# A chunked scan over image rows: TensorE's products regrouped, cumulative sums copied inside SBUF, statistics every fourth row

## The reference

```python
dA_cs = jnp.cumsum(dA, axis=2)
Lmat = jnp.exp(dA_cs[:, :, :, None, :] - dA_cs[:, :, None, :, :])
att = jnp.einsum('bcihn,bcjhn->bcijh', Ch, Bh) * Lmat * dtc[:, :, None, :, :]
att = jnp.where(causal[None, None, :, :, None], att, 0.0)
y_intra = jnp.einsum('bcijh,bcjhp->bcihp', att, xc)
states = jnp.einsum('bcjhn,bcjh,bcjhp->bchpn', Bh, decay_to_end * dtc, xc)
y_inter = jnp.einsum('bcihn,bcih,bchpn->bcihp', Ch, jnp.exp(dA_cs), prev_states)
```

## Time and profile before

| | us |
|---|---|
| median of 3 runs | 2463.56 (2460.02 to 2467.26) |
| profiled execution, its own time | 2459.31 |
| its span, first to last instruction | 2457.5 |
| the scan, first to last work on TensorE | about 858 to 1835 |

### The profile page before, as it was taken

How to read it: one execution, slowest core, us unless ns; L and a number is a source line. 1 busy time by engine, 2 the same in 40 slices (tenths; PEclk the granted TensorE clock), 3 DMA queues, 4 the chain that set the end, 5 groups by cost and what they waited for, 6 DMA issues and landing times. The chain is left out here.

```text
span 2457.5 us, 64304 instructions
## 1 busy us (share of the span) xinstructions
PE 2165.3 (88%) x22969; PEld 1624.6 (66%) x23096; DVE 1662.4 (68%) x3164; ACT 1311.9 (53%) x2727; POOL 1109.5 (45%) x1392
## 2 busy tenths in 40 slices
PE   0699997998899399999999999999987999879998
PEld 0475645887788267777777777777766656356563
DVE  5355585665565578888888888888873555735557
ACT  0255540085047577777777777777743555334543
POOL 0333250000000168888778877878853322432325
PEclk9999997999999699999999999999998999989999
DMA  9624495415623422222222222222226045961459
GB/s 215 182 81 79 100 329 160 122 29 179 204 54 125 137 51 60 60 58 58 58 61 59 61 58 58 58 59 60 59 60 180 25 88 139 311 184 35 91 132 316
DMA packets 305629, 272.25 MB, mean 111 GB/s; under 512 B 175966, under 2 KB 238846, under 8 KB 299210
## 3 DMA queue, kind: packets, MB, share of 16 engines
q1 hardware_dynamic: 294698, 256.00, 37.5%
q0 software_dynamic: 9280, 6.44, 2.1%
q10 hardware_dynamic: 1496, 7.63, 1.0%
HBM read 165.29 MB, written 81.46 MB: 100 GB/s over the span
## 5 line engine op out<-in xcount | busy, mean ns | idle before, releaser
L1692 DVE TENSOR_TENSOR l_scan_att<-l_scan_decay,l_scan_causal_scores 128x512 f32<-128x512 f32 x384 | 330.2, 860 | 63.3 <-ACT l_scan_decay L1661 63.1
L715 ACT COPY l_arena<-l_body_bank 128x384 f32<-128x384 f32 x192 | 142.0, 901 | 262.3 <-PE l_body_bank L587 262.3
L1655 ACT ACTIVATE l_scan_decay<-l_scan_cum 128x512 f32<-128x512 f32 x384 | 216.3, 597 | 33.0 <-PE l_scan_cum L1547 32.9
L1661 ACT ACTIVATE l_scan_decay<-l_scan_decay 128x512 f32<-128x512 f32 x384 | 227.8, 630 | 4.1
L1672 ACT ACTIVATE l_scan_yw<-l_scan_y_by_channel,l_scan_norm_b,l_scan_norm_w 128x128 f32<-128x128 f32 x384 | 148.1, 456 | 125.5 <-PE l_scan_y_by_channel L1609 124.5
L1594 PE MATMUL l_scan_gate_projected<-l_scan_xr,l_wf 97*128 97x128 f32 (+1 forms) x1536 | 205.3, 283 | 1.4 <-DVE l_scan_xo L1747 1.2
L1625 PE MATMUL l_scan_gate_projected<-l_scan_yz,l_scan_wo 128*96 128x128 f32 x1536 | 198.5, 279 | 1.1 <-DVE l_scan_yz L1724 1.1
L567 POOL TENSOR_TENSOR l_arena<-l_arena 96x512 f32<-96x512 f32 x96 | 122.6, 1277 | 168.8 <-ACT l_arena L780 161.6
L1625 PEld LDWEIGHTS l_scan_gate_projected<-l_scan_yz,l_scan_wo 128*96 128x96 f32 x1536 | 170.9, 163 | 40.0 <-issue 29.6
L1512 POOL TENSOR_TENSOR l_scan_inter<-l_scan_inter,l_scan_xd 128x384 f32<-128x384 f32 x128 | 128.0, 1000 | 151.4 <-DVE l_scan_inter L1707 151.4
L1594 PEld LDWEIGHTS l_scan_gate_projected<-l_scan_xr,l_wf 97*128 97x128 f32 (+1 forms) x1536 | 181.0, 190 | 17.2 <-issue 2.2
(11 more groups left out here) (191 smaller groups left out, 4896.2 us busy)
## 6 DMA issues: line engine op xcount, KB each, us to landing
l_scan_xc<-convolved_rows SPq DMA_DIRECT2D x128, 224.0 KB, 2.8
x_after<-l_arena SPq DMA_DIRECT2D x64, 384.0 KB, 4.8
l_arena<-x_after SPq DMA_DIRECT2D x64, 384.0 KB, 5.6
convolved_rows<-l_slots SPq DMA_DIRECT2D x48, 441.0 KB
l_conv_x_main<-x_after SPq DMA_DIRECT2D x64, 256.0 KB, 2.8
l_arena<-x_after SPq DMA_DIRECT2D x16, 1024.0 KB, 8.7
prepare_xt<-x SPq DMA_DIRECT2D x8, 1536.0 KB, 9.3
l_arena<-x SPq DMA_DIRECT2D x32, 384.0 KB, 5.5
```

Of the source, the lines that this page charges most:

```text
L715: nc.scalar.copy(tA[:, b, :, j:j + 2].rearrange("p c q -> p q c"), bank[n % 4][:, 0:2 * C].rearrange("p (q c) -> p q c", q=2)).then_inc(t_ ...
L1655: nc.scalar.activation(decay[:, b % 2, 4 * g:4 * g + 4, :], cum[(b + g) % 2][:], ACT.Relu, scale=-1.0)\
L1661: nc.scalar.activation(group, group, ACT.Exp, scale=-1.0).then_inc(exp_done, 1)
L1692: nc.vector.tensor_tensor(att[:, b, 4 * g:4 * g + 4, :], decay[:, b % 2, 4 * g:4 * g + 4, :], causal[:, b % 2:b % 2 + 1, :].broadcast_to([ ...
```

## The change

In `step_sizes` the unused columns of `parts` are filled with -1 instead of 0, and so the unused partitions of `cum_t` hold -1. `pick` and `unpick` go. In their place `lift` holds, for each of the four rows in flight, the spreading weights, and three further partitions of it get the row's own cumulative sums (three bf16 parts, 12 heads of 128) by three DMAs from `cum_t` to `lift` inside SBUF. The partitions of -1 multiply these, so that four products of 128 columns give both terms and L1544's product of 512 columns is gone. The first cumulative group of a row waits for the three DMAs of that row.

```diff
@@ -1275,7 +1275,7 @@
 
             @block.gpsimd
             def _(pool):
-                nc.gpsimd.memset(parts[:], 0.0).then_inc(padded, 1)
+                nc.gpsimd.memset(parts[:], -1.0).then_inc(padded, 1)
...
-        pick = ph.sb("pick", [128, 2 * N_HEADS, 128], BF16)
-        unpick = ph.sb("unpick", [128, 2 * N_HEADS, 128], BF16)
+        lift = ph.sb("lift", [128, U, N_HEADS, 128], BF16)
...
-        xo = ph.sb("xo", [CH, U, 2, W])
+        xo = ph.sb("xo", [CH, 2, U, W])
...
-        half_i = slice(0, D_INNER // 2)
+        half_i, half_s = slice(0, D_INNER // 2), slice(D_INNER // 2, D_INNER)
...
+        lift_landed = [ph.sem(f"own_cum_landed{b}") for b in range(U)]
...
                     sp.dma_start(tile[:], source).then_inc(ready, 16)
+                sp.wait_ge(ready, CONST)
...
@@ -1461,6 +1462,12 @@
                             .then_inc(xc_landed[b], 16)
                         sp.dma_start(xc[:, b, 0:CONV_DIM].rearrange("w (g c) -> w g c", g=8),
                                      xbc[:, :, bass.ds(r, 1), :].rearrange("g w o c -> w g (o c)")).then_inc(xc_landed[b], 16)
+                        if not (isinstance(r, int) and r < U):
+                            hold(sp, cum_done, 3 * (r - 3), passed)
+                        for part in range(3):
+                            own = 64 * (b % 2) + 3 * N_HEADS + part
+                            first = 64 * (b % 2) + part * N_HEADS
+                            sp.dma_start(lift[own:own + 1, b], cum_t[first:first + N_HEADS, bass.ds(n * 2 + b // 2, 1), :])                                .then_inc(lift_landed[b], 16)
...
-                    sp.dma_start(x_new[:, :, bass.ds(r * W, W)], xo[:, b]).then_inc(stored[b], 16)
+                    sp.dma_start(x_new[:, :, bass.ds(r * W, W)], xo[:, :, b]).then_inc(stored[b], 16)
...
                     pe.wait_ge(gap_done, q + 1)
-                    heads = slice((b % 2) * N_HEADS + 4 * g, (b % 2) * N_HEADS + 4 * g + 4)
-                    nc.tensor.matmul(bank[:].rearrange("p h w -> p (h w)"), pair, unpick[:, heads, :].rearrange("p h w -> p (h w)"),
-                                     start=True, stop=False)
+                    if g == 0:
+                        pe.wait_ge(lift_landed[b], n * 48 + 48)
                     for h in range(4):
-                        last = nc.tensor.matmul(bank[:, h, :], pick[:, (b % 2) * N_HEADS + 4 * g + h, :], pair,
-                                                start=False, stop=(h == 3))
+                        last = nc.tensor.matmul(bank[:, h, :], lift[:, b, 4 * g + h, :], pair, start=(h == 0), stop=(h == 3))
                     last.then_inc(cum_done, 1)
...
+                    if row0:
+                        cumulative(row0, 0)
+                        r, b, n = row0
+                        pe.wait_ge(xc_landed[b], n * 32 + 32)
+                        pe.wait_ge(masked, r + 1)
+                        nc.tensor.transpose(p_bcg[:, 0, :], xc[:, b, CONV_DIM + N_STATE - 128:], ident[:]).then_inc(bc_turned, 1)
                     if row2:
                         r, b, n = row2
                         pe.wait_ge(xs_ready, 3 * r + 3)
@@ -1564,25 +1575,21 @@
                                 last = nc.tensor.matmul(p_yt[h * HEAD:(h + 1) * HEAD, g, :], xdt[:, b % 2, head],
                                                         att[:, b, 4 * g + h, :], start=(g == 0), stop=(g == 2))
                         last.then_inc(yi_done, 1)
-                    if row0:
-                        r, b, n = row0
-                        pe.wait_ge(xc_landed[b], n * 32 + 32)
-                        pe.wait_ge(masked, r + 1)
-                        nc.tensor.transpose(p_bcg[:, 0, :], xc[:, b, CONV_DIM + N_STATE - 128:], ident[:]).then_inc(bc_turned, 1)
-                    if row2:
-                        r, b, n = row2
                         pe.wait_ge(state_ready, r + 1)
+                        for g in range(2):
+                            last = nc.tensor.matmul(p_i[g * N_STATE:(g + 1) * N_STATE, 0, half_s], xc[:, b, D_INNER:D_INNER + N_STATE],
+                                                    xw[:, b % 2, g * D_INNER // 2:(g + 1) * D_INNER // 2], start=True, stop=True)
+                        last.then_inc(st_done, 1)
                         for g in range(2):
                             at = slice(g * N_STATE, (g + 1) * N_STATE)
                             last = nc.tensor.matmul(p_i[:, g, half_i], bct[at, b, 1, :], state[at, :], start=True, stop=True)
                         last.then_inc(inter_done, 1)
...
                     if row0:
-                        cumulative(row0, 0)
-                        cumulative(row0, 1)
                         r, b, n = row0
                         pe.wait_ge(bc_copied, r + 1)
                         nc.tensor.matmul(p_bcg[:, 1, :], bct[0:N_STATE, b, 0, :], bct[0:N_STATE, b, 1, :], start=True, stop=True)\
                             .then_inc(scores, 1)
+                        cumulative(row0, 1)
...
                     if row0:
                         cumulative(row0, 2)
-                    if row2:
-                        r, b, n = row2
-                        pe.wait_ge(scaled, r + 1)
-                        for g in range(2):
-                            last = nc.tensor.matmul(p_i[g * N_STATE:(g + 1) * N_STATE, 0, half_i], xc[:, b, D_INNER:D_INNER + N_STATE],
-                                                    xw[:, b % 2, g * D_INNER // 2:(g + 1) * D_INNER // 2], start=True, stop=True)
-                        last.then_inc(st_done, 1)
                     if row4:
                         r, b, n = row4
...
+                    if row0:
+                        r, b, n = row0
+                        act.wait_ge(att_done, 3 * r)
+                        gaps(0)
+                        act.wait_ge(bc_turned, r + 1)
+                        if not (isinstance(r, int) and r < U):
+                            act.wait_ge(inter_done, r - 2)
+                        nc.scalar.copy(bct[0:N_STATE, b, 0, :], p_bcg[N_STATE:2 * N_STATE, 0, :])
+                        nc.scalar.copy(bct[:, b, 1, :], p_bcg[2 * N_STATE:4 * N_STATE, 0, :]).then_inc(bc_copied, 1)
                     if row2:
                         r, b, n = row2
                         act.wait_ge(yi_done, r + 2)
                         act.wait_ge(y_back, r)
                         nc.scalar.copy(yt[:], p_yt[:]).then_inc(yt_kept, 1)
...
                     if row0:
-                        r, b, n = row0
...
-                        gaps(0)
+                        decays(0)
                         gaps(1)
-                        decays(0)
                         decays(1)
...
-                nc.vector.tensor_copy(pick[:], spread(spreads[:], 128)).then_inc(ready, 1)
-                nc.vector.tensor_scalar(unpick[:], spread(spreads[:], 128), -1.0, None, ALU.mult).then_inc(ready, 1)
+                for b in range(U):
+                    heads = slice((b % 2) * N_HEADS, (b % 2 + 1) * N_HEADS)
+                    nc.vector.tensor_copy(lift[:, b], spread(spreads[:, heads], 128)).then_inc(ready, 1)
...
                         nc.vector.bn_stats(st6[:, b], y[:, b % 2]).then_inc(counted, 1)
                         hold(dve, counted, r + 1, passed)
                         nc.vector.bn_aggr(mv[:, b], st6[:, b]).then_inc(agg, 1)
+                        dve.wait_ge(st_done, r + 2)
+                        dve.wait_ge(faded_done, r + 1)
+                        nc.vector.tensor_tensor(state[:], p_i[0:2 * N_STATE, 0, half_s], faded[:], ALU.add).then_inc(state_ready, 1)
                     if row0:
                         attention(row0[0], row0[1], 1)
-                    if row2:
-                        r, b, n = row2
-                        dve.wait_ge(st_done, r + 2)
-                        dve.wait_ge(faded_done, r + 1)
-                        nc.vector.tensor_tensor(state[:], p_i[0:2 * N_STATE, 0, half_i], faded[:], ALU.add).then_inc(state_ready, 1)
+                    if row4:
+                        r, b, n = row4
+                        dve.wait_ge(o_done, r + 1)
+                        dve.wait_ge(stored[b], n * 16 + 16)
+                        nc.vector.tensor_tensor(xo[:, :, b], p_o[:], xr[0:CH, b], ALU.add).then_inc(xo_done, 1)
                     if row0:
                         attention(row0[0], row0[1], 2)
                     if row4:
                         r, b, n = row4
-                        dve.wait_ge(o_done, r + 1)
-                        dve.wait_ge(stored[b], n * 16 + 16)
-                        nc.vector.tensor_tensor(xo[:, b], p_o[:], xr[0:CH, b], ALU.add).then_inc(xo_done, 1)
                         dve.wait_ge(xo_done, r + 1)
-                        for kk in range(2):
-                            nc.vector.bn_stats(stats[:, kk, bass.ds(r, 1), :], xo[:, b, kk, :]).then_inc(stats_done, 1)
+                        if b == U - 1:
+                            for kk in range(2):
```

(3 more changed lines are left out.)

27 lines of the change are left out of this document (11 added, 16 removed).

## The result

The changed kernel takes 2439.35 us (median; 2431.08 to 2448.42), the kernel before beside it 2455.15 us (2443.23 to 2467.26). The ratio is 0.9945, with a 95% interval of 0.9929 to 0.9960: 13.5 us or 0.55% faster. I had said 3% faster, 74 us. The direction was right and the time lies inside the stated range, but four fifths of the gain did not come. The profiled execution of the changed kernel took 2444.79 us (span 2442.8), 14.5 less than that of before.

A forecast was written before the change was run, and what follows sets the result against it. TensorE's list was taken to bound the scan at 7.53 us a turn; 6.90 over about 124 rows gains 78 us, less 3.8 at the start: -74 us, 2390 us, range 2340 to 2450.

The forecast's parts named there:

- What bounds the kernel before: In the scan, TensorE's list of 7.53 us sets the turn; VectorE's 6.34, GpSimd's 5.97 and ScalarE's 5.41 have slack.
- TensorE's new list: In the scan, 6.28 less 0.66 for wide products plus 0.42 for three form changes: 6.04 us a turn.
- Chain E: Scan loop from GpSimd's add through three products, rstd's two steps, VectorE's yn and scaled: 6.6 to 6.9 us a turn.
- Chain G: In the scan, from xo through SP's copies, TensorE and VectorE over two turns: 13.35 us, so 6.7 a turn.
- The two together: In the scan, the two longest chains share engines and seldom fall into step: 6.9 us a turn taken.
- The statistics: VectorE's two statistics a row in the scan become a quarter of the instructions: 0.14 us a turn saved.
- The start: At the scan's start SP waits for the constants, then issues loads and copies that must land: +3.8 us once.
- The aggregate of the next layer: After the scan, it reads a quarter of the data, but VectorE idles 5.06 us before the next phase: gain 0.
- R2: Scan order couples badly, head-of-queue jitter paid by all engines: turn 7.15 to 7.43 us, 2420 to 2455 us; chance 0.20.
- R1: TensorE and VectorE alone decide the scan's turn: 6.4 to 6.6 us, 2327 to 2352 us; chance 0.15.
- R3: Slower than before, the scan's copies landing late at 3.6 us: turn 7.63 us, 2481 us; chance 0.10.
- R4: Scan's wide products gone but form changes kept: TensorE's list 6.87, turn near 7.15 us, 2420 us; chance inside R2's 0.20.

The follow-up runs named there:

- before_ynlater: The kernel before with VectorE's yn moved behind the scaled result, nothing else: 2462.31 us against 2449.02.
- best_nocopies: The changed kernel without copies, wide products kept, yn behind scaled, statistics every row: 2361.35 us, ratio to the kernel before 0.9633.
- nopow: early2 with rstd's second step, the power, left out, so the normalization's scale isn't computed: 2373.48 us.
- early2: The changed kernel with the copies of the next row issued behind the xc loads of this one, a turn earlier: 2435.59 us.
- ynlater: The changed kernel with VectorE's yn moved from ahead of the scaled result to behind it: 2452.59 us.
- reorder: The changed kernel without the copies, wide products and their constant tables as before, all else as changed: 2421.46 us (2448.08 beside it).
- best_copies: The changed kernel with copies a turn earlier behind the xc loads, yn behind scaled, statistics every row: 2360.04 us, ratio to the kernel before 0.9637.
- ynlater_early2: The changed kernel with yn behind scaled and the copies one turn earlier behind the xc loads: 2377.92 us.
- rowstats: The changed kernel with the statistics of xo taken every row over 128 elements again: 2442.58 us.
- xdlast: The changed kernel with GpSimd's product xd moved behind rstd, TensorE's intra product no longer waiting for it: 2469.71 us (2450.3 beside it).
- early: The changed kernel with the three copies of a row issued one SP turn earlier, ahead of the xc loads: 2538.08 us, 2450.3 beside it.

## Why the prediction was wrong, point by point

**What bounds the kernel before: right.** TensorE's list, 7.53 us. before_ynlater moved nothing.

**TensorE's new list: right to about 0.1 us, the shares by luck.** The gap between inter products and scores is gone. Where TensorE is full again and keeps the wide products (best_nocopies), its turn is 6.77 against 6.70 by the terms of my sum; and a group without its wide product takes 0.23 us from its start to that of the next product (1311.14 to 1311.37 in the changed kernel), where the sum had 0.22. The stretch after shows TensorE at 88.8 of 100 us (I had said 87 to 90), VectorE at 90.0 (near 90), GpSimd at 85.4 (near 86). But these shares belong to a turn of 7.34 where I expected 6.9: busy time a turn is 6.5, 6.6 and 6.3 us, where the sum had 6.0, 6.2 and 6.0. For VectorE and GpSimd, instructions beside each other grew: yn from 0.46 to 0.81, rstd's second step from 1.12 to 1.19, its first from 0.51 to 0.66 (medians over 1000 to 1700 us). That the shares came out as forecast is no evidence for the turn.

**Chain E: the step that failed.** I took 6.6 to 6.9 us a turn for it; it measures 7.21 to 7.24. Against the upper figure, my 6.93, the turn of 7.24 splits so: from the add to the end of rstd 1306.86 to 1312.62 is 5.76, where I had 5.66; yn and scaled take 1.28, where I had 0.93; yn wakes after 0.03, where I had 0.17; then 0.17 as before. So the term that was mis-sized is yn and scaled, +0.35 us. I had read it from a turn in which the statistics held yn back until GpSimd had nearly finished its copy and faded product. Once yn hangs on rstd it starts together with them, and takes 0.81 us instead of 0.46. The lower figure, 6.6, failed for a second reason. It used the mean of GpSimd's instructions, as if a mean over turns that do not hang on the chain could be the chain's length. The means of the six that the chain goes through (add, three products, two steps of rstd) sum to 5.50 us before and 5.79 in the changed kernel, where xdt takes 1.28 and rstd's second step 1.19 in every turn, as they do beside an attention product. My least value, near 5.5, does not follow from the one row that I named for it: that row takes 0.56 off 6.93, and the rest comes from other rows of the last turns. By nopow and by early2 this chain alone holds the turn at 7.21.

The rule of the Trainium skill that I had weighed, "GPSIMD Engine Reference", section "Specifications", that VectorE's instructions with two SBUF inputs share GpSimd's SBUF interface, spoke against the lower end, and the runs agree with it: rstd's second step took 1.19 us in the steady state and, before the change, 0.57 in the last turns, its first 1.69 beside two attention products.

**Chain G: also too short, by the issue of the copies.** I took 6.7 us a turn, and 5.7 us of it from the end of xo to TensorE's start; that measures 1304.35 to 1311.14, 6.79. The third issue starts at 1309.05 (1307.19 + 2.60 less its own 0.74), 4.70 after xo, where I had 3.84: the issue of one copy holds SP for 0.74 to 0.81 us and the next stands 0.90 to 0.96 behind it, where I had carried the 0.40 and 0.54 of the xc loads over. From that issue to TensorE are 2.09 us; with my 0.17 for waking the landing is 1.9, where I had 1.7. With 6.79 in place of 5.7 my sum gives 14.4 for two turns, 7.2 a turn; ynlater's rows give 14.54 and 15.0. The rest of the sum is right in size and not in its path: from TensorE's start to yz I had 4.15 through the gate, and there it is 4.52 through the inter products, the scaled result, yn and the first attention product; from yz to the end of xo it is 3.23 where I had 3.50.

The Trainium skill's fixed 2.0 us ("DMA: Bandwidth & Descriptors", section "Anatomy of one DMA"), which the page gives for the GpSimd path, is nearer to this landing than my 1.7. Most of the miss was in the issue, though.

**The two together.** From 6.7 and 6.6 to 6.9 I took a turn of 6.9. Chain E was 0.3 us longer than its upper figure and chain G 0.5 longer than its own, and the turn is 7.34.

**The statistics: wrong sign.** I had them at -0.14 us a turn. As two instructions of 0.67 us in one turn of four they fill that turn: early2 and reorder have 7.52 in the turn that has them and 7.21 to 7.25 in the others, +0.3 (no run took the grouping alone out of these two), and best_copies against ynlater_early2 shows 0.56 over four turns. In the changed kernel itself they cost nothing that shows. Spread over the rows they fit into the 0.47 us in which VectorE waits for rstd anyway, and rowstats shows it: VectorE busier by 3 of 100 us, the four turns no longer.

**The start: too low.** I had +3.8 us. TensorE's first work comes 9.90 us after the scan's first instruction instead of 5.90, +4.0, nearly as said. But then it does not catch up: the first turns have to wait for SP, which issues ten DMAs for two rows where it issued four. SP's issues at the start:

```profile
851.12 0.33 SPq L1461 DMA_DIRECT2D l_scan_xc<-convolved_rows  x1
851.50 0.43 SPq L1463 DMA_DIRECT2D l_scan_xc<-convolved_rows  x1
851.97 2.48 SPq L1470 DMA_DIRECT2D l_scan_lift<-l_cum  x3
854.49 0.51 SPq L1461 DMA_DIRECT2D l_scan_xc<-convolved_rows  x1
```

and the first adds on GpSimd:

```profile
868.52 1.00 POOL L1519 TENSOR_TENSOR l_scan_inter<-l_scan_inter,l_scan_xd 128x384 f32<-128x384 f32 x1 [10.97 <-DVE l_scan_inter L1709]
877.20 1.00 POOL L1519 TENSOR_TENSOR l_scan_inter<-l_scan_inter,l_scan_xd 128x384 f32<-128x384 f32 x1 [2.07 <-DVE l_scan_inter L1709]
885.51 0.99 POOL L1519 TENSOR_TENSOR l_scan_inter<-l_scan_inter,l_scan_xd 128x384 f32<-128x384 f32 x1 [1.90 <-DVE l_scan_inter L1709]
894.64 1.00 POOL L1519 TENSOR_TENSOR l_scan_inter<-l_scan_inter,l_scan_xd 128x384 f32<-128x384 f32 x1 [0.68 <-DVE l_scan_inter L1709]
```

From SP's first issue of the scan (846.42) to the fourth add are 48.2 us; before it was 37.3 (852.81 to 890.09). So the start costs 10.9 us. In reorder it is 41.6 (840.47 to 882.04): 4.3 of it come with the new order, 6.6 with the copies and SP's wait for the constants. With the turns the sum closes: from the fourth add to the last are 932.5 us before and 910.0 now, 22.5 less; less 10.9 at the start and 0.6 behind the last add that is 11.0, what the scan is shorter by.

**The aggregate of the next layer: right, nearly.** It fell from two of 3.59 us to two of 0.99, 5.2 less, and VectorE's idle time behind it grew by about as much, from 5.06 to 10.14:

```profile
1820.23 1.90 DVE L289 BATCH_NORM_AGGREGATE l_fold_mv<-row_stats 96x2 f32<-96x192 f32 x2 [1.76 <-PEq L74]
...
1835.70 1.92 DVE L798 TENSOR_SCALAR l_arena<-l_arena,l_scales 128x512 f32<-128x512 f32 x4 [10.14 <-PEq L74]
```

From the scan's last instruction to this work are 17.2 us instead of 18.1. I had said 0.

**The rivals.** R2's numbers are what came, 7.15 to 7.43 us a turn against 7.34, and 2420 to 2455 us. I gave it 0.20 and wrote against it that no chain I could add up reached it. Two do, both of them my own, with 0.3 us more in E and 0.5 more in G. That the time fell inside R2's band, and inside the stated range, is therefore no credit to the working. Of its mechanism, jitter that every engine pays for, the runs show nothing: the turns repeat to 0.01 us. R1 and R3 did not come; the landing of R3, 3.4 us, was 1.9. R4 did not come.

**What stays open.** The slow fourth turn is 7.7 in the changed kernel and in rowstats, where the statistics are spread; it is 7.52 without the wait for the copies. So copies and statistics each can make it, but how the two chains fall into step to give just 7.7 was not told apart. Nor was it tried to issue the copies from another queue than SP's.

## What to carry to other kernels

When a change takes work off the engine that is full, look in the trace for the other closed loops, from a release to the same release one turn later. The interval in the trace is the loop's length only where each step starts as the one before it ends. Where a step waits for something else, as yn did for the statistics, find what it will run beside once it doesn't: here yn and scaled took 0.35 us more for it, most of what the sum lacked. An engine's mean busy time is not a chain. Price a DMA by its issue as well as its landing, since the queue behind it waits for the issue. Where undoing one suspect gains nothing, undo two together before acquitting it.

## What the runs showed of the hardware

- GpSimd's instructions on a single element in each partition take longer beside VectorE's attention product, which has two inputs in SBUF: here from two to over seven times as long. The first step of rstd took 0.22 us without one beside it, 0.66 (median) in the changed kernel and 1.69 beside two of them (xdlast); the power took 0.57 and 1.19. The product xdt took 0.83 without and 1.28 with one beside it, and the attention product took 1.39 beside the add and xdt and 0.67 where neither ran.
- VectorE's yn took 0.81 us where it started together with GpSimd's copy and faded product, and 0.46 where it started behind them (the fourth turn of early2). Where it started ahead of the faded product (nopow) it took 0.47 and the faded product 0.67 instead of 0.50.
- The issue of a copy inside SBUF that fills one partition takes 0.75 us (median of 384) on SP's queue, the loads from HBM on the same queue 0.35 to 0.41. TensorE starts on it 2.1 us after the issue starts.
- Where TensorE idled 1 to 2 us in most turns (early) its granted clock was between 0.93 and 0.97 of its upper level in these stretches; in the changed kernel, whose longest wait for the copies is 0.9 us, and in ynlater, with up to 1.4 us in one turn of two, it was 1.00.
